# Order of work in an attention loop: score groups by token half, the first average before the routing prefix, the state last, and a weight split moved on GpSimd

## The reference

```python
q, k, v = split(layernorm(h) @ w_inp + b_inp)
qf = exp(q @ omega - diag_q - max_q) + EPS         # 16 features a head
kf = exp(k @ omega - diag_k - max_k) + EPS
a  = causal sum over earlier tokens s of (qf[t] . kf[s]) * v[s]
h  = h + (a / (the same sum without v)) @ w_out + b_out
```

## Time and profile before

| What | us |
|---|---|
| Median of 3 runs | 883.47 (881.82 to 892.5) |
| The profiled execution | 889.71 |
| Its span, first to last instruction | 887.9 |
| TensorE busy | 710.2 (80%) |
| VectorE, ScalarE, GpSimd busy | 512.0, 439.4, 433.9 |
| Mean granted TensorE clock | 0.86 of full |
| Attention loop, iterations 3 to 15 | 283.97 |

### The profile page before, as it was taken

How to read it: one execution, slowest core, us unless ns; L and a number is a source line. 1 busy time by engine, 2 the same in 40 slices (tenths; PEclk the granted TensorE clock), 3 DMA queues, 4 the chain that set the end, 5 groups by cost and what they waited for, 6 DMA issues and landing times. The chain is left out here.

```text
span 887.9 us, 17124 instructions
## 1 busy us (share of the span) xinstructions
PE 710.2 (80%) x4943; PEld 663.2 (75%) x4944; DVE 512.0 (58%) x1472; ACT 439.4 (49%) x853; POOL 433.9 (49%) x457
## 2 busy tenths in 40 slices
PE   2663279989999999999986049999996999999950
PEld 1353268888888888888886049999996999999950
DVE  1542025756666677676753247888799565656520
ACT  1431045545555555555540137777773666566630
POOL 7761022424444445444432336777774766665443
PEclk9688558968888899898975569999999999999995
DMA  8924100111111111111110023333332334343337
GB/s 213 235 46 157 54 23 14 53 35 44 43 43 43 43 43 52 43 43 43 34 34 22 8 50 54 57 60 58 59 59 43 47 77 71 81 74 78 57 45 142
DMA packets 60016, 55.08 MB, mean 62 GB/s; under 512 B 24232, under 2 KB 51311, under 8 KB 59967
## 3 DMA queue, kind: packets, MB, share of 16 engines
q0 software_dynamic: 19840, 23.53, 15.6%
q1 hardware_dynamic: 35647, 27.76, 11.9%
q10 hardware_dynamic: 4480, 3.21, 1.1%
HBM read 32.52 MB, written 25.10 MB: 65 GB/s over the span
## 5 line engine op out<-in xcount | busy, mean ns | idle before, releaser
L1139 POOL DMA_INDIRECT result<-e_y,e_tag x78 | 138.3, 1773 | 96.9 <-DVE e_y L1469 85.0
L1198 PE MATMUL e_yp<-x_w2s,e_hh 128*128 x468 | 139.4, 365 | 2.0 <-DVE e_y L1469 2.0
L1462 DVE TENSOR_TENSOR e_hl<-e_hid,e_hh 128x512 fp32r<-128x512 f32 x117 | 80.3, 690 | 88.9 <-ACT e_hh L1264 88.6
L502 POOL DMA_INDIRECT tbl_dram<-a_entry,a_slot x64 | 63.1, 986 | 132.1 <-DVE a_entry L985 104.4
L1256 ACT ACTIVATE e_hid<-e_hidden,e_b 128x256 f32<-128x256 f32 x234 | 100.8, 474 | 53.8 <-PE e_hidden L1185 39.2
L1199 PE MATMUL e_yp<-x_w2s,e_hl 128*128 x468 | 117.5, 251 | 0.0
L585 PE MATMUL a_ab<-a_values,a_masked 128*128 (+1 forms) x768 | 113.6, 297 | 0.0
L585 PEld LDWEIGHTS a_ab<-a_values,a_masked 128*128 128x128 f32 x768 | 108.0, 216 | 5.0 <-issue 4.3
L1264 ACT CAST e_hh<-e_hid 128x512 fp32r<-128x512 f32 x117 | 72.4, 621 | 62.0 <-PE e_yp L1199 62.0
L1127 POOL DMA_INDIRECT e_x<-x_dram,e_tag x78 | 80.9, 1037 | 37.8 <-issue 22.9
L1198 PEld LDWEIGHTS e_yp<-x_w2s,e_hh 128*128 128x128 f32 x468 | 87.9, 188 | 2.5 <-issue 2.3
(11 more groups left out here) (252 smaller groups left out, 1623.8 us busy)
## 6 DMA issues: line engine op xcount, KB each, us to landing
a_raw<-in_ew SPq DMA_DIRECT2D x16, 288.0 KB, 2.8
t_hs<-in_ew SPq DMA_DIRECT2D x8, 384.0 KB, 9.3
t_hs<-in_ew SPq DMA_DIRECT2D x16, 192.0 KB, 10.1
h_dram<-t_hs SPq DMA_DIRECT2D x4, 768.0 KB, 4.2
a_hb<-h_dram SPq DMA_DIRECT2D x16, 192.0 KB, 2.4
result<-a_hb SPq DMA_DIRECT2D x16, 192.0 KB, 4.1
x_dram<-a_att SPq DMA_DIRECT2D x16, 192.0 KB, 2.1
spec_dram<-e_space ACTq DMA_DIRECT2D x16, 192.0 KB, 1.9
```

The lines of the kernel that those rows point to most:

```text
L1139: pool.indirect_dma_start(out=out, in_=y[:, j], in_offset=None, out_offset=bass.IndirectOffsetOnAxis(ap=tag[:, i % 8, j, 0:1].bitcast(U32) ...
L1198: pe.matmul(Y[:, j, 0:2 * D], hh[:, f, c], w(f, 2 * D), start=f == 0, stop=False, skip_group_check=True)
L1462: g.tensor_tensor(hl[:, f:f + 2].rearrange("p f t -> p (f t)"), hid[:, f:f + 2].rearrange("p f t -> p (f t)"), hh[:, f:f + 2].rearrange("p ...
```

## The change

Five edits, all in `attention_block`:

1. Score groups go by token half: groups 0 to 2 are half 0, groups 3 to 5 are half 1. S and the masked tiles go by n % 2 as before. Only groups 0 and 3 wait for the transposed keys and queries of their half, and ScalarE's overwriting of half j waits for groups up to 3(j + 1).
2. average(0) stands ahead of the prefix on TensorE, and mask(1) ahead of `place` on VectorE.
3. The state's matmuls stand last in the iteration on TensorE, behind the features' and queries' transposes of half 1.
4. The state's masking on VectorE moves from the iteration's end to the next iteration, between mask(0) and mask(1), as `take_state`.
5. On GpSimd the low part of the expert weights stands right behind rstd2, ahead of `low_part(i, 0)`.

```diff
--- before.py
+++ after.py
@@ -506,13 +506,13 @@
                 if tail:
                     rstd("rstd2_ready", i - 2, mv2, rstd2, "tail", 5 * (i - 2) + 4)
                 if one:
+                    wait_apart(pool, s["high"], i + 1)
+                    v = lambda c: w2s[:, bass.ds(i, 1), :, c * D:(c + 1) * D].rearrange("k u f d -> k (u f) d")
+                    g.tensor_tensor(v(1), raw[:], v(0).bitcast(F32), ALU.subtract).then_inc(s["low"], 1)
                     low_part(i, 0)
                     if not (fixed(i) and i == B - 1):
                         rstd("rstd1_ready", i + 1, mv, rstd1, "norm_step", 5 * (i + 1) + 4)
                     low_part(i, 1)
-                    wait_apart(pool, s["high"], i + 1)
-                    v = lambda c: w2s[:, bass.ds(i, 1), :, c * D:(c + 1) * D].rearrange("k u f d -> k (u f) d")
-                    g.tensor_tensor(v(1), raw[:], v(0).bitcast(F32), ALU.subtract).then_inc(s["low"], 1)
             sched(pool, emit)
             pool.wait_ge(s["scattered"], 16 * 4 * B)
 
@@ -551,14 +551,14 @@
 
                 def score(n):
 
-                    g, j = n // 2, n % 2
-                    if n < 2:
+                    j, g = n // NG, n % NG
+                    if g == 0:
                         pe.wait_ge(s["kT_out"], TJ * b + j + 1)
                         pe.wait_ge(s["qT_out"], TJ * b + j + 1)
                     if not (fixed(i) and i == 1) or n >= 2:
                         pe.wait_ge(s["s_out"], 6 * b + n - 1)
                     for p in range(2):
-                        last = pe.matmul(S[j][:, 2 * p:2 * p + 2].rearrange("p h t -> p (h t)"),
+                        last = pe.matmul(S[n % 2][:, 2 * p:2 * p + 2].rearrange("p h t -> p (h t)"),
                                          kf_t[:, 2 * g + p, j * P:(j + 1) * P],
                                          qb_t[:, 2 * g + p, j].rearrange("p h t -> p (h t)"), start=True, stop=True)
                     last.then_inc(s["s_done"], 1)
@@ -582,7 +582,7 @@
                     for r in range(GH):
                         h = j * H + g * GH + r
                         own_and_zeros = values[:, (i + 1) % 2, h:TJ * H + 1:TJ * H - h]
-                        last = pe.matmul(beside(o + r * VW), masked[j][:, r],
+                        last = pe.matmul(beside(o + r * VW), masked[n % 2][:, r],
                                          own_and_zeros.unsqueeze(1).broadcast_to([P, 2, 2, VW]),
                                          start=n == 0 and r == 0, stop=True, skip_group_check=True)
                     last.then_inc(s["av_done"], 1)
@@ -614,6 +614,8 @@
                     pe.wait_ge(s["att_ready"], i - 1)
                     pe.wait_ge(s["kT_out"], TJ * known(i))
                     turn(R[2], att).then_inc(s["attT_done"], 1)
+                if two:
+                    average(0)
                 if choice:
                     pe.wait_ge(s["chosen_ready"], i - 2)
                     if not fixed(i) or i >= 4:
@@ -625,8 +627,6 @@
                     for j in range(TJ):
                         pe.matmul(all_of, ones[:], count[:, j].unsqueeze(1).broadcast_to([P, TJ, NE]), start=False, stop=False)
                     pe.matmul(M[:, NE:2 * NE], ones[:], chosen[:, 0], start=False, stop=True).then_inc(s["prefix_done"], 1)
-                if two:
-                    average(0)
                 if one:
                     pe.wait_ge(s["xn_ready"], i + 1)
                     if not (fixed(i) and i == 0):
@@ -704,6 +704,13 @@
                 if two:
                     average(5)
                 if one:
+                    pe.wait_ge(s["qT_out"], TJ * i + 1)
+                    for c in range(2):
+                        last = pe.transpose(FA[0:CF, NP * P + c * P:NP * P + (c + 1) * P],
+                                            feat[1][:, c * HC:(c + 1) * HC].rearrange("p h f -> p (h f)"), ident[:])
+                    last.then_inc(s["qf_done"], 1)
+                    turn_queries(1)
+                if one:
                     if not (fixed(i) and i == 0):
                         pe.wait_ge(s["state_out"], i)
                     if tail:
@@ -714,13 +721,6 @@
                                          values[:, i % 2, c * HC:(c + 1) * HC].rearrange("p h v -> p (h v)"),
                                          start=True, stop=True)
                     last.then_inc(s["state_done"], 1)
-                if one:
-                    pe.wait_ge(s["qT_out"], TJ * i + 1)
-                    for c in range(2):
-                        last = pe.transpose(FA[0:CF, NP * P + c * P:NP * P + (c + 1) * P],
-                                            feat[1][:, c * HC:(c + 1) * HC].rearrange("p h f -> p (h f)"), ident[:])
-                    last.then_inc(s["qf_done"], 1)
-                    turn_queries(1)
             sched(pe, emit)
 
         @block.scalar
@@ -752,14 +752,14 @@
                 def keys_out(j):
                     act.wait_ge(s["kT_done"], TJ * i + j + 1)
                     if two:
-                        act.wait_ge(s["s_done"], 6 * b + 5 + j)
+                        act.wait_ge(s["s_done"], 6 * b + NG * (j + 1))
                     act.copy(kf_t[:, :, j * P:(j + 1) * P], FB[0:CF, 0:NP * P].rearrange("p (n t) -> p n t", n=NP)
                              ).then_inc(s["kT_out"], 1)
 
                 def queries_out(j):
                     act.wait_ge(s["qT_done"], TJ * i + j + 1)
                     if two:
-                        act.wait_ge(s["s_done"], 6 * b + 5 + j)
+                        act.wait_ge(s["s_done"], 6 * b + NG * (j + 1))
                     for r in range(2):
                         last = act.activation(qb_t[:, :, j, r], FA[0:CF, 0:NP * P].rearrange("p (n t) -> p n t", n=NP),
                                               ACT.Copy, scale=own_head[:, r:r + 1])
@@ -869,10 +869,11 @@
                 more = one and not (fixed(i) and i == B - 1)
                 if two:
                     mask(i, 0)
+                    take_state(i - 1)
+                if two:
+                    mask(i, 1)
                 if choice:
                     place(i - 3)
-                if two:
-                    mask(i, 1)
                 if tail:
                     project(i - 2)
                 if one:
@@ -899,13 +900,14 @@
                     apply1(i + 1)
                 if two:
                     normalise(i - 1)
-                if one:
-                    dve.wait_ge(s["state_done"], i + 1)
-                    if two:
-                        dve.wait_ge(s["av_done"], 6 * (i - 1) + 2)
-                    v.tensor_tensor(state[:], M[0:CF, 0:2 * CV].rearrange("p (c x) -> p c x", c=2),
-                                    block_mask[:].rearrange("p h v -> p (h v)").unsqueeze(1).broadcast_to([CF, 2, CV]),
-                                    ALU.mult).then_inc(s["state_out"], 1)
+
+            def take_state(b):
+                dve.wait_ge(s["state_done"], b + 1)
+                if not fixed(b) or b >= 1:
+                    dve.wait_ge(s["av_done"], 6 * (b - 1) + 2)
+                v.tensor_tensor(state[:], M[0:CF, 0:2 * CV].rearrange("p (c x) -> p c x", c=2),
+                                block_mask[:].rearrange("p h v -> p (h v)").unsqueeze(1).broadcast_to([CF, 2, CV]),
+                                ALU.mult).then_inc(s["state_out"], 1)
 
             def normalise(b):
                 ab = AB[:].rearrange("p (j x) -> p j x", j=TJ)[:, :, 0:H * VW].rearrange("p j (h v) -> p j h v", v=VW)
```

## The result

| | before | after |
|---|---|---|
| Median | 887.99 us (4 runs, 881.82 to 895.06) | 949.43 us (4 runs, 947.56 to 953.78) |
| Profiled execution (its span) | 889.71 (887.9) | 953.78 (952.1) |
| Mean granted clock | 0.86 | 0.80 |

The ratio is 1.0724, 95% interval [1.0626, 1.0821]: slower, as forecast, but by 61 us instead of 24.5, and outside the range. Before has one execution more here than the three shown ahead of the prediction.

The account below looks back on a forecast made before the run. Bound by TensorE, 80% busy, with the routing chain to xn2 as second limit. Seven kind A and six kind B iterations make 314.5 against 283.97 us (+30.5); the edges give -6; 883.47 + 24.5 = 908 us, range 862 to 926.

Parts of the forecast that it names:

- Top stall: TensorE's 1.53 us idle time between score(0) and score(1), waiting for ScalarE's queries of the second token half, goes away.
- scores by half: Score(0) and score(1) both need only half 0, so TensorE is ready for average(0) at 1.20 us at the latest.
- state last: Mask(0) no longer stands behind the state but still waits for normalise and score(0); average(0) gains only 0.2 us.
- Prefix and place: Prefix starts 2.15 us after score(0) instead of 2.74, so place and all that hangs on it gain 0.59 us.
- The hold of norm2: On VectorE, norm2 is held by GpSimd's 1.41 us weights' low part: 1.4 us later, TensorE stalling 2.6 us before xn2.
- The gain at `choose`: L961 on VectorE, no longer beside the weights' low part, gains 1.15 us, worth at most 0.1 because normalise waits for average(5).
- the idle time at xn2 costs the clock: After the stall before the xn2 transposes TensorE falls to half clock; the second half takes 13.64 us instead of 8.33.
- Kind B: Six of thirteen loop iterations: half-clock head of 8.9 us, TensorE late, nearly no stall left at xn2; 22.2 us each.
- kind A: Seven of thirteen loop iterations: full clock to xn2 (12.3 us), then 13.6 us at low clock; 25.9 us each.
- The last rival: Half clock in nearly every loop iteration, a stall at xn2 in each: 28.0 us each, 957 us; chance 0.06.
- The edges: Iterations 1 and 2 and the tail, outside the thirteen loop iterations, only gain: together -6 us.
- The rival without a hold: Norm2 not held, 1.2 us stall at xn2 still lowers the clock, in turn or every third iteration: 890 us; chance 0.17.

Follow-up runs that it names:

- the filler's run: The kernel after with four unread matmuls of 408 columns on TensorE ahead of its wait for xn2 in each full loop iteration: 869.95 us, ratio 0.9806.
- prefix first: The kernel after with the weights' low part last again, prefix ahead of average(0) and place ahead of mask(1), as in before: ratio 0.9501.
- half the filler: The kernel after with two unread matmuls of 408 columns instead of four ahead of TensorE's wait for xn2: 892.44 us, ratio 0.9976.

## Why the prediction was wrong in size

**Top stall, scores by half, state last: right.** No idle time at score(1), and the iteration ahead of the pattern fell by 4.7 us to 17.75, forecast 4.

**Prefix and place: right.** The prefix started 2.75 us after score(0) and not 2.15, because the head ran at the low clock (348.58 - 346.73 = 1.85 to average(0)). From the prefix to the end of rstd2 it took 8.04 us; forecast 0.28 + 1.83 + 5.91 = 8.02.

**The hold of norm2: right.** 2.02 us against 2.07, and a stall of 2.54 us against 2.6. The Trainium skill (SBUF — State Buffer, section "SBUF: two separate sides") has the shared port pair kept for whole instructions; the trace agrees, with a pair that grew by 1.35 us beside one 1.39 us operation. The full-clock period of 20.66 was 20.92 in the filler's run. The gain at `choose` (0.17 us instead of 1.32) was hidden, as forecast: VectorE's first operation of `normalise` then waited 4.54 us for average(5).

**That the idle time at xn2 costs the clock: right.** The filler's run shows it: the same edits, no idle time at xn2, clock 1.00 in all loop iterations. The Trainium skill (TensorE: Matmul & The Clock Gate, section "Why this matters for your kernels") would have had no fall from gaps as short as these; the trace disagrees, with 0.73 over thirteen iterations whose longest idle time is 2.58 us.

**Kind B: the step that failed.** I had a half-clock head of 8.9 us follow each iteration of kind A, which would make TensorE late and leave nearly no stall at xn2. I took that length from iteration 4 of before (194.06 to 203.00), which still had a stall at its top; the change removes just this stall. It ended 2 us into that head:

```profile
196.09 0.77 PE L561 MATMUL a_s<-a_qb_t,a_kf_t 96*128 96x256 f32 x2 [1.29 <-issue]
```

The run with the groups alternating again brought the top stall back, and with it the alternation, 26.0 to 28.0 and 23.5 to 23.9 us. In after the clock was back by 348.58, 1.9 us into the head, TensorE was early again, and the 2.54 us came back in twelve of thirteen iterations. The last rival, at 957 us and a chance of 0.06, had this by its number, and I argued against it with the very head that the change alters. By its mechanism it was right only in part: it had the head slow throughout and a stall behind it all the same, while the head was slow for 1.9 us alone.

**Kind A was too short as well**, 27.3 us on average against 25.9. Its head took 12.90 us instead of 12.3 (346.73 to 359.63; the slow start above), and its second half 14.1 to 15.5 (387.96 to 402.02, 359.63 to 375.08) against 13.64: in iteration 3 of before the clock fell 2.2 us behind the stall, here in five cases of twelve before the stall had ended. The sum: five more A in place of B, 5 x (25.9 - 22.2) = 18.5; twelve A at 1.4 more, 16.5; one B at 0.5 more. Together 35.5, and 314.5 + 35.5 is the measured 350. So the missing kind B and the length of kind A weigh about the same.

**The edges** brought 1.9 us instead of 6, but the attention's part of them brought 7.9. The other 6.0 went in the block behind it, which the change doesn't touch. From the attention's last xn2 to the end, before and then after:

```profile
485.51:887.90 402.39, 323.55 (x2423) 317.44 (x2423) 246.57 (x608) 219.93 (x474) 233.39 (x181) 0.91 0.36 62
```

```profile
543.67:952.10 408.43, 331.04 (x2423) 325.14 (x2423) 246.91 (x608) 220.57 (x474) 235.44 (x181) 0.89 0.36 62
```

The same instructions took longer at a slightly lower clock. In six other profiled runs (edit 5 undone, edit 5 alone, both fillers, alternating groups, prefix first) this stretch takes 401.8 to 405.4 us. So it looks like a matter of this one execution, the slowest of the four, which the runs do not prove. The stall at xn2 of the tail's first iteration is longer, 5.80 us (521.94) where before has 1.95 (463.78), but that is no loss of its size: from score(0) to those transposes it is 11.96 us against 11.67. TensorE only comes earlier to the same wait.

**The rival without a hold** (1.2 us of stall, 890 us) was wrong for the change without edit 5: 930 us, because L490 holds norm2 too once TensorE is early, and the stall is 1.87 us. But where the stall really was 1.13 us, with half the filler, four iterations of thirteen lost the clock, near the "every third" that this rival had as one of its two cases, and the kernel stood at the time of before.

## What to carry to other kernels

Before you remove a stall of TensorE, find the next wait that TensorE will reach early and take that chain out of the way first: the same edits gave 7% more time with the chain in place and 6 to 7% less once one GpSimd step was moved past two DMAs. Where iterations with a low clock are used as a pattern, check that the stall which shaped them is still there after the change. And when busy time of TensorE grows with its count of matmuls unchanged, fill the idle time with unread matmuls in one run: it separates the price of the wait from that of the clock.

## What was not expected of the hardware

Adding two or four idle-filling matmuls an iteration took the ratio to before from 1.072 to 0.998 and to 0.981. A stall of 1.13 us in front of the same work lowered the clock in four iterations of thirteen, and one of 1.87 us in ten of twelve. After such a stall TensorE stayed at 1.2 GHz through a second half in which it was busy all the time; this window of after begins at the stall's end:

```profile
359.63:374.00 14.37, 14.37 (x74) 14.33 (x74) 6.42 (x26) 6.02 (x10) 2.44 (x5) 0.50 0.19 52
```

Then it came back 0.8 to 3.1 us into the next head in 24 cases of 26 (after, edit 5 undone, half the filler), and 7 to 9 us into it in all six where an idle time of 0.61 us stood there (alternating groups). The two other cases of the 26 took over 7 us with no idle time in the head. What in the work decides when it comes back stays open; the runs show only that idle time in the head delays it. Last, one program had two steady periods in two executions on two chips, 18.88 and 18.16 us at full clock, by 0.74 us of VectorE idle time for which the profile names no cause that would differ.
